# One block from the pair attention to the output, and the linear attention's keys centred in one VectorE pass

## What is computed

```python
# layer 2, attention: one head, keys and queries relu(. @ W.T + b) of the normalised x and of the context,
#   softmax over the 64 context tokens of the sequence, values are the context itself
# layer 2, feed-forward: 8 experts, the best 2 of each token
logits = (x @ gate_w + gate_b) / 0.9            # x normalised
out = sum over the 2 best experts of prob * (gelu(x @ w1 + b1) @ w2 + b2)
out = layernorm(out) * ln_g + ln_b
# layer 3, attention: linear, 8 heads of 64; each key row joins a learned null key and null value
k = softmax over the head's features of the keys (with the null key's), context = k^T v, out = softmax(q) context
out = layernorm(out) @ Wout
# layer 3, feed-forward: 8 experts, the best 2, capacity 1.25, silu(x @ W1) * (x @ W3) @ W2
```

## Time and profile before

| | us |
|---|---|
| median of 3 runs | 1663.19 |
| lowest and highest run | 1657.54, 1663.44 |
| the profiled execution's own time | 1652.23 |
| its span, first to last instruction | 1650.5 |
| PE busy in the span | 1235.0 |
| DVE busy | 956.0 |
| POOL busy | 850.6 |
| ACT busy | 731.6 |

### The profile page before, as it was taken

The page is one execution under the profiler, slowest core; times in us unless marked ns, Lnnn a source line. Parts: engine busy times, 40 slices in busy tenths (PEclk is TensorE's granted clock), DMA queues, the critical chain, the costliest instruction groups (busy, mean ns, idle before and its releaser), DMA issues. The chain is left out here.

```text
span 1650.5 us, 36142 instructions
## 1 busy us (share of the span) xinstructions
PE 1235.0 (75%) x11766; PEld 996.3 (60%) x11766; DVE 956.0 (58%) x2772; ACT 731.6 (44%) x1774; POOL 850.6 (52%) x1123
## 2 busy tenths in 40 slices
PE   3888883863888689655339997598888836999991
PEld 2677663762767557444328886366666634888880
DVE  3877672227899767457712223599898832444444
ACT  2765551322788535344214444466555521222222
POOL 1355656343777323645624444677898761333334
PEclk9987785885999879777569999799999967999996
DMA  5322200744333100201157776100000012222215
GB/s 135 105 81 88 77 23 22 199 132 117 104 104 106 38 1 1 70 12 40 65 153 201 211 210 162 35 2 7 17 19 17 17 35 79 74 64 63 76 35 157
DMA packets 156238, 130.06 MB, mean 79 GB/s; under 512 B 21530, under 2 KB 133932, under 8 KB 156080
## 3 DMA queue, kind: packets, MB, share of 16 engines
q1 hardware_dynamic: 142672, 105.23, 22.6%
q0 software_dynamic: 11264, 21.07, 3.8%
q10 hardware_dynamic: 2144, 1.75, 0.4%
HBM read 89.77 MB, written 40.57 MB: 79 GB/s over the span
## 5 line engine op out<-in xcount | busy, mean ns | idle before, releaser
L1342 POOL DMA_INDIRECT l_rows_out<-l3e_y,l3e_target x80 | 77.7, 971 | 176.1 <-DVE l3e_y L1330 163.9
L1298 ACT ACTIVATE l3e_sT<-l3e_ps_h 128x256 f32<-128x256 f32 x160 | 61.3, 383 | 177.7 <-PE l3e_ps_h L1269 149.8
L1342 POOL DMA_INDIRECT l_rows_out<-l2e_y,l2e_target x80 | 77.8, 972 | 99.7 <-DVE l2e_y L1328 87.5
L1316 DVE TENSOR_TENSOR l3e_hT<-l3e_sT,l3e_ps_h 128x256 f32<-128x256 f32 x160 | 67.4, 421 | 98.9 <-ACT l3e_sT L1298 98.9
L1295 ACT ACTIVATE l2e_hT<-l2e_ps_h,l2e_b 128x256 f32<-128x256 f32 x160 | 69.9, 473 | 95.2 <-PE l2e_ps_h L1264 95.2
L1268 PE MATMUL l3e_ps_h<-l3e_xT,l3e_w 128*128 128x256 f32 x320 | 100.8, 397 | 4.9 <-DVE l3e_xT L1307 0.6
L1269 PE MATMUL l3e_ps_h<-l3e_xT,l3e_w 128*128 128x256 f32 x320 | 96.2, 383 | 0.0
L1066 POOL DMA_INDIRECT l_rows_in<-l2a_rt_rows,l2f_slot x64 | 62.8, 982 | 58.2 <-DVE l2f_slot L1056 40.8
L1278 PE MATMUL l2e_ps_y<-l2e_w,l2e_hT 128*128 128x128 f32 x640 | 78.3, 276 | 0.0
L1278 PE MATMUL l3e_ps_y<-l3e_w,l3e_hT 128*128 128x128 f32 x640 | 78.0, 275 | 0.0
L1264 PE MATMUL l2e_ps_h<-l2e_xT,l2e_w 128*128 128x256 f32 x320 | 77.6, 386 | 0.6 <-DVE l2e_xT L1307 0.6
(11 more groups left out here) (524 smaller groups left out, 3761.9 us busy)
## 6 DMA issues: line engine op xcount, KB each, us to landing
l2e_w<-in_L_ffn_w SPq DMA_DIRECT2D x80, 256.0 KB
l1a_side<-in_fside_Bx16xSxS SPq DMA_DIRECT2D x32, 512.0 KB, 3.6
l0e_w<-in_L_ffn_w SPq DMA_DIRECT2D x32, 256.0 KB
l_rows_in<-l0a_fill_rows SPq DMA_DIRECT2D x14, 528.0 KB, 2.7
l_rows_out<-l0a_fill_rows SPq DMA_DIRECT2D x12, 512.0 KB, 3.5
l3e_w<-in_L_ffn_W SPq DMA_DIRECT2D x24, 256.0 KB
l2e_rows<-l_rows_in SPq DMA_DIRECT2D x40, 132.0 KB, 3.2
l3e_rows<-l_rows_in SPq DMA_DIRECT2D x40, 132.0 KB, 2.2
```

The source lines that it names most:

```text
L1298: nc.scalar.activation(sT[:, f % 2, :], ps_h[f % 2][:, 0:CHUNK], act_func).then_inc(s_ready, 1)
L1316: nc.vector.tensor_tensor(hT[:, b, f, :], sT[:, f % 2, :], ps_h[2 + f % 2][:, 0:CHUNK], ALU.mult).then_inc(h_ready, 1)
L1342: pool.indirect_dma_start(out=r.rows_out, out_offset=bass.IndirectOffsetOnAxis(ap=target[:, c % 2, a:a + 1], axis=0), in_=y[:, c % 2, a, : ...
```

## The change

The four stages l2a, l2e with l3a, l3e and l3c become one block in one Phase (`pairs_to_end`). Semaphores are shared among steps and handed from one part to the next so that they suffice; the second use of a semaphore waits for its value plus what the first reached.

- The ends of l2a, l3a and l3e have no barrier any more. PE waits for the few results that free its PSUM (`psum_free`), SP for the scatters (`rows_sent`), each in its own stream.
- SP waits for `allotted` (DVE's table of chunks), then issues the weight sets 0 to 3 of the layer 2 experts, then waits for the scatters and the filled ends, then issues the rows of chunks 0 to 3, and then the layer 3 attention's 12 weight DMAs, which ACT issued before. The gains' two DMAs now come before all others of l2a.
- In layer 3, SP issues the first 2 weight sets once the layer 2 results are added into x, then waits for the scatters, then issues the rows.
- In l2a the context for the values comes in one DMA instead of 4 (CX), DVE makes the first 4 tiles of xn instead of POOL, before its masks, and the router's work on a quad comes one iteration later on PE, ACT and DVE, in a loop with one iteration more.
- In l3a, L2499 and L2502 become one `scalar_tensor_tensor`, and ACT gets one operation more for each tile.

The core of the diff (the experts' waits are only renamed to go through `passed` and `freed`, and are left out; so are the joined semaphores' new numbers):

```diff
-            for t in range(NT):
+        for t in range(G, NT):
                 pool.tensor_scalar(xn[:, t, :], core.x[:, t, :], core.mean[:, t:t + 1], core.rstd[:, t:t + 1],
...
-            for i in range(-3, NSTEP + 2):
+        for i in range(-3, NSTEP + 3):
                 scores(i + 1)
                 project_context(i + 3)
-                router.positions(pe, i - 2, ps_l[:, 256:512])
+            router.positions(pe, i - 3, ps_l[:, 256:512])
                 turn_p(i)
                 turn_x(i + 2)
                 values(i)
                 project(i + 2)
-                router.logits(pe, i - 1, ps_l)
-                router.turn(pe, i, ps_r)
+            router.logits(pe, i - 2, ps_l)
+            router.turn(pe, i - 1, ps_r)
...
+            router.normalise(act, i - 1)
                 context(i + 3)
-                router.normalise(act, i)
-                router.turned(act, i, ps_r)
+            router.turned(act, i - 1, ps_r)
...
             root_on_vector(dve)
+        for t in range(G):
+            V.tensor_scalar(xn[:, t, :], core.x[:, t, :], core.mean[:, t:t + 1], core.rstd[:, t:t + 1], ALU.subtract, ALU.mult
+                            ).then_inc(s["first_ready"], 1)
...
-                router.slots(dve, i - 2, ps_l[:, 256:512])
+            router.slots(dve, i - 3, ps_l[:, 256:512])
                 residual(i)
                 router.statistics(dve, i, s["summed"])
-                router.read(dve, i - 1, ps_l)
-                router.choose(dve, i - 1)
-                router.prefix(dve, i - 1)
+            router.read(dve, i - 2, ps_l)
+            router.choose(dve, i - 2)
+            router.prefix(dve, i - 2)
...
         def one(u, c):
-            if c % inner == 0:
-                load_set(u, c // inner)
+            ahead = rows_ready is not None and isinstance(u, int) and u == 0
+            if ahead and c == 0:
+                for k in range(BUFS):
+                    load_set(u, k)
+                rows_ready(sp)
+            if not ahead and c % inner == 0:
+                load_set(u, c // inner)
+            load_rows(u, c)
+            if ahead and c == STEP - 1 and behind_first is not None:
+                behind_first(sp)
...
+        def null_exponents(t):
+            if not is_tile(t):
+                return
+            act.wait_ge(s["mk_ready"], t + 1)
+            reused(act, s["ek_ready"], 2 * t)
+            nc.scalar.activation(above[:, :], nmk0[:, t % 2, :], ACT.Relu, bias=nnk[:, :], scale=-1.0).then_inc(s["above_ready"], 1)
...
-            nc.scalar.activation(ek[:, I:I + H], nmk[:, :], ACT.Exp, bias=nk[:, :]).then_inc(s["ek_ready"], 1)
+            nc.scalar.activation(ek[:, I:I + H], above[:, :], ACT.Exp, scale=-1.0).then_inc(s["ek_ready"], 1)
...
-            V.tensor_scalar(nmk[:, :], nmk0[:, :], nnk[:, :], None, ALU.min).then_inc(s["mk_ready"], 1)
             dve.wait_ge(s["mk_ready"], t + 1)
             reused(dve, s["ek_ready"], 2 * t - 1)
-            V.tensor_tensor(kc[:, :].rearrange("p (c k) -> p c k", k=S), ps_kv[:, :].rearrange("p (c k) -> p c k", k=S),
-                            nmk[:, :].unsqueeze(2).broadcast_to([P, H, S]), ALU.add).then_inc(s["kc_ready"], 1)
+            V.scalar_tensor_tensor(out=kc[:, :].rearrange("p (c k) -> p c k", k=S), in0=nmk0[:, t % 2, :].unsqueeze(2).broadcast_to([P, H, S]),
+                                   scalar=nnk[:, :], in1=ps_kv[:, :].rearrange("p (c k) -> p c k", k=S), op0=ALU.min, op1=ALU.add
+                                   ).then_inc(s["kc_ready"], 1)
...
+        @block.sync
+        def _(sp):
+            combine.load_gains(sp)
+            pairs.sync(sp)
+            sp.wait_ge(allotted, 1)
+
+            def load_weights(sp):
+                pairs_done(sp)
+                weights(sp)
+            expert.sync(sp, rows_ready=rows_in, behind_first=load_weights)
             all_stored(sp)
             combine.load_rows(sp)
+            sp.wait_ge(combine.s["added"], combine.NQ)
+            third.sync(sp, rows_ready=rows_sent)
+            third_stored(sp)
+            last.sync(sp)
```

More of the change, by code:

```diff
@@ L634, in _ @@
                 router.single_weights(dve, route_gate)
-def combine_and_store(nc, core, name, r, out):
+class LastCombine:
     GROUP = 4
     NG = NT // GROUP
[L644 to L666, removed]
-            for t in range(NT):
[L668 to L682, removed]
-                dve.wait_ge(added, t + 1)
-                nc.vector.scalar_tensor_tensor(out=core.x[:, t, :], in0=got[:, 0, t, :], scalar=r.weight[:, 0, t:t + 1], in1=core.x[:, t, :],
-                                               op0=ALU.mult, op1=ALU.add).then_inc(x_ready, 1)
@@ new lines, in scalar, with gpsimd @@
+    def scalar(self, act):
+        for t in range(NT):
+            if t % self.GROUP == 0:
+                act.wait_ge(self.rows_arrived[t // self.GROUP], self.rows_base + 32)
+            self.nc.scalar.activation(self.part[:, t, :], self.got[:, 1, t, :], ACT.Copy, scale=self.r.weight[:, 1, t:t + 1]
+                                      ).then_inc(self.scaled, 1)
+    def gpsimd(self, pool):
+        for t in range(NT):
+            pool.wait_ge(self.scaled, self.scaled_base + t + 1)
+            pool.tensor_tensor(self.core.x[:, t, :], self.core.x[:, t, :], self.part[:, t, :], ALU.add).then_inc(self.added, 1)
@@ new lines, in vector @@
+    def vector(self, dve):
+        for t in range(NT):
+            if t % self.GROUP == 0:
+                dve.wait_ge(self.rows_arrived[t // self.GROUP], self.rows_base + 32)
+            dve.wait_ge(self.added, self.added_base + t + 1)
+            self.nc.vector.scalar_tensor_tensor(out=self.core.x[:, t, :], in0=self.got[:, 0, t, :], scalar=self.r.weight[:, 0, t:t + 1],
+                                                in1=self.core.x[:, t, :], op0=ALU.mult, op1=ALU.add).then_inc(self.x_ready, 1)
@@ new lines, in pair_programs, with is_step, sync @@
+    cx_in = [ph.sem(f"cx_in{k}") for k in range(CX)]
+    root_on_vector, nmr_ready = statistics(nc, ph, core)
+    def is_step(c):
+        return 0 <= c < NSTEP
+    def sync(sp):
+        sp.dma_start(wT[:, :], wT_dram).then_inc(s["w_in"], 16)
+        sp.dma_start(b[:, :], b_dram.rearrange("(r a) -> r a", a=1)).then_inc(s["w_in"], 16)
+        src = pad_dram.rearrange("(a b) k -> a (b k)", a=1)
+        sp.dma_start(pad[:, :, :, :].rearrange("p b n k -> p (b n k)"), src.broadcast_to([P, NT * P])).then_inc(s["pad_in"], 16)
+        ctx_tiles = flat(ctx_dram).rearrange("(n p) d -> p n d", p=P)
+        for k in range(CX):
+            part = slice(k * NT // CX, (k + 1) * NT // CX)
+            sp.dma_start(cx[:, part, :], ctx_tiles[:, part, :]).then_inc(cx_in[k], 16)
+        router.load(sp)
+        router.fill_tails(sp)
@@ L2665, in _ @@
             attention.vector(dve)
+            third.vector(dve)
+            last.vector(dve)
         @block.gpsimd
```

766 lines of the change are left out of this document (412 added, 354 removed).

## The result

The changed kernel takes 1633.74 us (median of 4 runs, 1630.72 to 1635.69), the kernel before 1660.37 (4 runs, 1653.84 to 1663.44): the ratio is 0.9843, with a 95% interval of 0.9811 to 0.9874. It is 26 us faster, inside the range given, but little more than half of the 48 us forecast. The same kernel timed again beside the experiments, with 6 runs each time, gave 0.9774 [0.9731, 0.9817] and 0.9769 [0.9731, 0.9806]: 37 to 38 us of the 1644 that the kernel before took there. So two questions are open: what the first pair of traces shows, and which terms of the 48 fell short.

What follows compares the result with a forecast made beforehand. PE fills both expert stages, so only the gaps ahead, SP's start in l2e and l3a's keys could shrink: 7.5 + 8.6 + 22 + 10 = 48 us off 1663.19 gives 1615; forecast 1607 to 1621, range 1595 to 1638.

Steps and rivals of the forecast that it cites:

- (b): Rival: l2a's loop gains nothing because steps stay at 13 us; 1625 to 1633 us, chance 0.15.
- (a): Rival: l3a's new keys give nothing because PE and POOL hold the iteration; 38 us gained, 1625 us, chance 0.17.
- The end of l3e: Last scatter of l3e to SP's first load: 9.67 us becomes 2.18, gaining 7.5, all on the path; bounds 6 to 8.
- The end of l3a: Last scatter of l3a to PE in l3e: 5.9 us in place of 14.5, gaining 8.6; bounds 7 to 10.
- The end of l2a: Last scatter of l2a to PE in l2e: 6.7 us in place of 20.68, gaining 14.0; lower bound 9.3.
- The loop of l2a: Moving the router one iteration later removes DVE's waits for scores; l2a's last scatter starts 8.4 us earlier.
- SP in l2e: SP decides l2e, so its weight set 4, 21 to 22 us earlier, counts; 22 us taken, bounds 9 to 27.
- The keys: In l3a, fusing L2499 and L2502 saves 0.67 us per tile on DVE; 10 us taken, bounds -9 to +21.
- (d): Rival: the keys of l3a give all their saving; 1605 us or less, chance 0.13.
- (e): Rival: shorter PE pauses lower the granted clock in l2e and l3e; 0.87 costs 53 us; chance 0.03.
- The four tiles and the context's DMA: In l2a, DVE's first 4 tiles of xn: no gain counted, -4 to +1.8 us; one context DMA: nothing.
- (c): Rival: gaps at the stage ends are landing, not barrier; some 15 us missing, 1630 us, chance 0.05.

Runs made afterwards that it cites:

- e1: The changed kernel unaltered, timed and traced a second time against the kernel before: ratio 0.9774.
- e6: The changed kernel with the router's work of l2a an iteration earlier, as it was before; ratio to the kernel before 0.9819.
- e9: The changed kernel unaltered, for a third trace, timed against the kernel before: ratio 0.9769.
- e4: The kernel before with only the new keys of l3a and no other part of the change; ratio to the kernel before 0.9950.
- e8: The changed kernel with the last combine (l3c) in a Phase and block of its own, so a barrier behind l3e; ratio to the kernel before 0.9763.
- e7: The changed kernel with both expert stages' first weight sets issued behind the wait for the scatters, between the rows; ratio to the kernel before 0.9863.
- e5: The changed kernel with DVE's shift of x waiting until all 64 scatters of l2a have landed; ratio to the kernel before 0.9763.
- e11: The changed kernel with layer 3's attention weights issued by ACT and DVE's shift of x behind l2a's scatters; ratio to the kernel before 0.9773.
- e10: The changed kernel with layer 3's twelve attention weight loads issued by ACT behind l2a's scatters, not SP; ratio to the kernel before 0.9786.
- e12: The changed kernel with l2a's first four normalised tiles made by POOL again in place of DVE; ratio to the kernel before 0.9773.

## Why the prediction came out as it did

Term by term in us gained, the first trace and e1 beside what was forecast; the terms of a column add up to the last row:

| | forecast | first trace | e1 |
|---|---|---|---|
| l2a, to its last scatter | 8.4 | 1.0 | 3.9 |
| last scatter to PE in l2e | 14.0 | -3.3 | 13.5 |
| l2e from PE's start | 0 | -9.1 | -2.0 |
| l3a | 10 | 8.8 | 4.6 |
| last scatter to PE in l3e | 8.6 | 9.8 | 9.8 |
| l3e | 0 | 0.1 | -0.6 |
| l3e to the load of l3c | 7.5 | 7.5 | 7.5 |
| from there to the end | 0 | -4.6 | -4.0 |
| sum | 48 | 10.2 | 32.7 |

The number came out inside the range, but not for the forecast's reasons alone. 1633.74 lies outside 1607 to 1621 and next to rival (b)'s 1625 to 1633, whose mechanism e6 excludes. The first trace has a disturbance of 27 us in it that nobody forecast, and a range that was drawn for other reasons was wide enough to hold it. Without that disturbance e1 and e9 are worth 32 to 38 us, where rival (a) stood, and (a)'s mechanism, keys that give nothing, is excluded by e4. What fell short in them are four terms: l2a by 4.5, l3a by 5.4, the end of the program by 4.0 and l2e by 2.0.

**The end of l3e: half right.** 7.5 was measured to the tenth. "All on the path, since nothing else runs there" was wrong: 4 come back at the end of the span. I had read the gap as the price of a barrier, to be struck out, and never asked what the end of the program costs with the longer block ahead of it. e8 shows both halves: of that gap SP spends 5.4 and 1.4 us on PE's sequencer, and in the merged kernel 3.4 and 1.4 of it come back at the last L73 and L76.

**The end of l3a: right**, 9.8 for 8.6 within its bounds. e7 puts the value of the early sets at 3.8 there. My estimate that the sets could cost 1.4 at most was too low: with two sets behind the landing PE starts 8.5 us behind the last scatter, not 7.3 (5.9 and 1.4).

**The end of l2a: right in e1**, by two errors that cancel. PE starts 7.15 behind the last scatter, forecast 6.7. But the landing doesn't take 2.18: POOL's next operation behind its wait comes 4.2 us behind the scatter's start (822.32 to 826.47). In the nine merged traces with sets issued ahead and no slow hand-overs it is 3.1 to 6.4, most where SP's sets run on past the last scatter (e5, e6, e11), and 2.5 in e7, where no set is under way. So SP issues rows 4.9 behind the last scatter, against my sign of under 3. The rows then need 2.3 to PE, not 3.7.

**The loop of l2a: the size was right, "free" was wrong.** e6 against e1 prices the router's shift at 7.1 for the last scatter and 8.0 for PE's start (10.3 and 11.3 against e9); I had 8.4. The slots of quad 5 come 115.9 us behind l2a's start in e1, forecast 115.5. The place where it fell short is the sentence that DVE's shift of x "stood in the barrier's shadow and now stands behind `allot` and the scatters, while SP and PE wait; free". It stands behind `allot`, but beside the scatters, eight of which are still to come, and it stops POOL for 4.2 us. e5 takes that out, and the last scatter stands 9.2 ahead of before. I had read the Trainium skill's rule on this very port pair for L2499 and for xn, and had not gone through all DVE operations that the change moves beside POOL's.

**SP in l2e: right.** Set 4 comes 17.9 earlier in e1, PE's start 17.4, l2e's last scatter 15.4. What set 4 lacks of the forecast 21 to 22 is about the 4.2 of the hole. From set 4 on l2e takes 160.1 in e1 against 157.7 before, a loss that I had at nothing; with the attention's weights on ACT (e10, e11) it is 157.2 and 157.3, but e4, with them on ACT too, has 159.3, so its cause stays open. e7 shows that SP's start on set 4 is what l2e's end follows. e10 shows the other side, that with these buffers it doesn't come sooner than 9 us behind PE's start.

**The keys: right**, 8.2 at equal clock for the 10 taken, between the rivals (a) and (d). In the merged kernel the traces give 2.0 to 8.8 by l3a's length, with mean granted clocks of 0.91 in the first trace and 0.88 in e1 and e9. In nine of the eleven traces with the new keys and the later joins l3a's clock is 0.88 or 0.89, where e4 and the kernel before had 0.90. That may be rival (e) on a small scale; no run takes it apart. The two expert stages kept 0.99 in e1 and e9, so (e) as it was told is out. One reading of the earlier trace rows was wrong as well: POOL leaves 9.84 - 8.48 = 1.4 us of an iteration with a quad, not 0.9. With 12 for PE and 11 for POOL the cap is no longer 19 but all 21.3 of L2499; half of that is 10.7, so the term hardly changes.

**The four tiles and the context's DMA:** no gain from the tiles, as forecast (e12). The context's DMA no run tests by itself.

**What the first 26 us are made of.** By the ratios e1 and e9 give 37 us, by the medians 32 and 35, and the parts above explain 33 of them in a trace. The first result stands up to 11 us lower, and its trace shows slow hand-overs from the middle of l2a (steps of up to 14.6 us between slots, where e1 has at most 12.8) to the end of l2e, worth 27 us from l2a's start to l2e's last scatter. Only one of its four runs was traced, but the other three point the same way: they took 1633 to 1636 us at mean granted clocks of 0.870 to 0.873, and e1's runs at 0.869 to 0.875 took 1608 to 1615. So it was hardly one execution alone. The kernel before was slower on that occasion too, 1660 against 1644 and 1641 beside the experiments, though its trace shows no slow hand-overs. The interval of the first ratio overlaps e1's by a hair and e9's not at all. The cause stays open. Nothing speaks for one that the change brings: the slow hand-overs are absent in the twelve traces that followed, ten of which have l2a and l2e in one block.

Of the rivals, (b), the loop, is out by e6; (c), landing and not barrier, is out but for the 2 us that the landing grew by; (a) and (d) are the two ends of what e4 measured in the middle.

## What to carry to other kernels

When a barrier goes, list every operation that stood in its shadow on each engine, and look at what it now runs beside: a large DVE operation with its operands in SBUF stops POOL's scatters for its whole length, and one wait moved it out of the way (e5: 4.2 us for the scatters, 3 for PE's start; by ratio, 0.9763, not to be told from the changed kernel). A saved barrier may come back at the next one, so count from the last join to the end of the span. And before two traces are subtracted, count each stage from its own start: here the code ahead of the change moved by up to 18 us between traces, much of it with the granted clock.

## What the runs showed of the hardware that I had not expected

- Hand-overs can be slow for a whole stretch: 1.2 us from one DVE operation to the next in place of 0.02 to 0.2, SP's eight tail DMAs in 21.7 us in place of 8.1, in one of 14 traces.
- The large DVE operation (128x4096, 4.43 us) turned a POOL scatter of 0.97 us into 5.16, and an `affine_select` of 0.29 into 4.30. A memset beside it kept its 0.10.
- A scatter's landing takes 2.2 to 2.5 us alone and 3.1 to 6.4 beside four weight sets (4 times 578 KB).
- At the end of the merged block SP waits 3.4 us for PE's sequencer, though PE has been idle for over 25; with the last combine in a block apart it waits 5.4 at the end of the block ahead and 0.2 at the end of the short one.
